# A mixer kernel's gated output projection, moved from a stage at the end into the scan loop

## What is computed

```
xz = x_seq @ W_in
x, z = (xz[..., :D_INNER], xz[..., D_INNER:])
x = _silu(_causal_conv(x, conv_w, conv_b))
proj = x @ W_xproj
dt = jax.nn.softplus(proj[..., :DT_RANK] @ W_dt + b_dt)
y = _selective_scan(x, dt, Bm, Cm, A, D)
return y * _silu(z) @ W_out
```

## Time and profile before

| | |
|---|---|
| median of 3 runs | 6110.16 us (6106.02 to 6110.85) |
| the profiled execution | 6104.23 us |
| its span | 6102.4 us |
| DVE busy | 5353.6 us, 88% of the span |
| POOL busy | 4946.7 us, 81% |
| PE busy | 4730.4 us, 78% |
| ACT busy | 3221.6 us, 53% |
| mean granted clock of PE | 0.734 |
| DVE busy tenths in 40 slices | 3224729999999999999999999999999999999953 |
| DMA, mean | 172 GB/s |

### The profile page before, as it was taken

One profiled execution on the slowest core, in us unless ns is written; L12 is line 12 of the kernel. 1 busy time (PEld: TensorE's weight loads), 2 busy tenths in 40 slices (PEclk: granted clock), 3 DMA queues, 4 the chain that ended last, 5 costly groups with the idle time before them and its releaser, 6 DMA issues. The chain is left out here.

```text
span 6102.4 us, 74088 instructions
## 1 busy us (share of the span) xinstructions
PE 4730.4 (78%) x17356; PEld 1206.1 (20%) x17356; DVE 5353.6 (88%) x3584; ACT 3221.6 (53%) x5155; POOL 4946.7 (81%) x2339
## 2 busy tenths in 40 slices
PE   7999737777777777777777777777777777777788
PEld 6776211111111111111111111111111111111122
DVE  3224729999999999999999999999999999999953
ACT  1226635555555555555555555555555555555533
POOL 0000429999999999999999999999999999999965
PEclk9999877666666666666666666666666676666689
DMA  1002745555555555555555555555555555555599
GB/s 34 27 27 82 224 122 182 183 183 183 183 181 182 181 180 179 184 179 182 180 182 180 181 181 182 181 181 181 182 183 183 183 183 183 183 183 183 183 263 273
DMA packets 351021, 1048.26 MB, mean 172 GB/s; under 512 B 66820, under 2 KB 101430, under 8 KB 300556
## 3 DMA queue, kind: packets, MB, share of 16 engines
q1 hardware_dynamic: 334976, 1022.36, 52.8%
q10 hardware_dynamic: 16012, 25.53, 1.3%
HBM read 836.01 MB, written 211.63 MB: 172 GB/s over the span
## 5 line engine op out<-in xcount | busy, mean ns | idle before, releaser
L1267 POOL TENSOR_TENSOR hc<-hring,c_rep 128x1024 f32<-128x1024 f32 x1539 | 3602.2, 2356 | 245.8 <-DVE hring L1230 235.2
L1230 DVE TENSOR_TENSOR_SCAN hring<-decay,carry,u_ps 128x1024 f32<-128x1024 f32 x1283 | 2971.8, 2333 | 0.0
L1035 PE MATMUL u_ps<-stack_b,w_spread 48*128 48x512 bf16 x2568 | 1117.4, 527 | 953.0 <-DVE hring L1230 951.8
L1125 ACT ACTIVATE decay<-dt_rep,w_a 128x1024 f32<-128x1024 f32 x1285 | 1469.8, 1146 | 571.0 <-DVE hring L1230 570.1
L1212 DVE TENSOR_TENSOR u_ps<-u_ps,u_rep 128x1024 f32<-128x1024 f32 x1284 | 1551.4, 1208 | 92.6 <-PE u_ps L1035 89.3
L1053 PE MATMUL y_ps<-hc,w_gather 128*32 128x512 f32 x6144 | 1170.8, 846 | 55.3 <-POOL hc L1267 55.3
L1125 ACT ACTIVATE u_ps<-dt_rep,w_a 128x1024 f32<-128x1024 f32 x257 | 287.4, 1118 | 979.4 <-DVE hring L1230 979.4
L1077 PE MATMUL prep_ps<-xn,w_conv 128*128 128x512 f32 x792 | 618.8, 875 | 73.0 <-DMA xn<-xn_scr 71.4
L1035 PEld LDWEIGHTS u_ps<-stack_b,w_spread 48*128 48x128 bf16 x2568 | 155.6, 102 | 2536.9 <-DVE hring L1230 1823.3
L582 POOL TENSOR_TENSOR xs<-xc_ln,rs 96x512 f32<-96x512 f32 x64 | 90.3, 1411 | 682.5 <-ACT rs L566 668.2
L1254 POOL TENSOR_TENSOR drive_p<-u_rep,b_rep 128x1024 f32<-128x1024 f32 x258 | 609.1, 2361 | 27.7 <-DMA u_rep<-u_scr 27.7
(11 more groups left out here) (108 smaller groups left out, 3926.8 us busy)
## 6 DMA issues: line engine op xcount, KB each, us to landing
dt_rep<-dt_scr SPq DMA_DIRECT2D x194, 1024.0 KB, 5.9
u_rep<-u_scr SPq DMA_DIRECT2D x194, 1024.0 KB, 7.9
c_rep<-bc_scr SPq DMA_DIRECT2D x260, 512.0 KB, 5.4
b_rep<-bc_scr SPq DMA_DIRECT2D x130, 512.0 KB, 4.4
xn<-xn_scr SPq DMA_DIRECT2D x132, 384.0 KB, 6.5
y_scr<-y_sb SPq DMA_DIRECT2D x768, 64.0 KB, 4.3
xn<-xn_scr SPq DMA_DIRECT2D x132, 256.0 KB, 6.7
dt_scr<-dt_sb SPq DMA_DIRECT2D x260, 128.0 KB, 2.1
```

The source lines that it names most:

```text
L1035: mm = nc.tensor.matmul(u_ps[nv % NSLOT][:, sl], w["spread"][:, q, :], upper(stack_b[drv][:, sl]), start=True, stop=True)
L1125: nc.scalar.activation(to[:, :], dt_rep[r][:, b, :], ACT.Exp, scale=w["a"][:, col:col + 1]).then_inc(decay_ready, 1)
L1230: nc.vector.tensor_tensor_scan(hring[nv % NHR][:, ::step], factor[:, ::step], term[:, ::step], carry[:, drv, nv:nv + 1], ALU.mult, ALU.add ...
L1267: nc.gpsimd.tensor_tensor(hc[nv % NHC][:, :], hring[nv % NHR][:, :], c_rep[q][:, :], ALU.mult).then_inc(c_applied, 1)
```

## The change

The scan loop gets two more tasks, `gate` and `slice`. In pass p (from p = 8, so from the second image on) they make one slice of the previous image's output: 56 slices in the passes 8 to 63. At step 14 of pass p-1 SP issues seven loads of slice p-8 (L1062 to L1066 of the new file; 983 KB). At steps 21 and 22 PE makes z into `prep_ps` and ACT copies it to `z_sb`. In pass p, at step 0 ACT takes the silu of z, at step 1 DVE adds the two y, at step 3 DVE multiplies, at step 7 PE projects (four float32 matmuls of 256 columns), at step 8 ACT copies the result and at step 10 SP stores it. The slice is laid out as 128 partitions by 768, as the scan's own channels are. `CONV_AT` moves by one step, so that the projection may use `prep_ps` at steps 7 and 8. The loop is split: three iterations without the new tasks, one unrolled iteration with the first z, 28 iterations with all of it. `output` keeps its form but runs over the last image's eight slices only (`over_last`). `weights` gains two matrices, with five more loads, a memset and three copies. The core of the diff:

```diff
-        CONV_AT = ((8, 9, 10), (12, 13, 14), (16, 17, 18))
+        CONV_AT = ((9, 10, 11), (13, 14, 15), (17, 18, 19))
...
+        SLICE_AT, Z_AT = 14, (21, 22)
+        SUM_Y_AT, GATE_AT, PROJECT_AT, RES_AT, OUT_STORE_AT = 1, 3, 7, 8, 10
+        SLICE_DMAS = 7
...
+        OUT_LAG = 2 * CHUNKS
+
+        def slice_of(it):
+
+            return it // CHUNKS - 1, (it + 1) % CHUNKS * T
...
+
+
+            with eng.Fori(0, CHUNKS - 1) as it:
+                iteration(it, (False, False), (False, False))
+            iteration(CHUNKS - 1, (False, True), (False, False))
+            with eng.Fori(CHUNKS, ITERS) as it:
+                iteration(it, (True, True), (True, True))
...
+                def gate(m, k, it, dr):
+                    if m == SLICE_AT:
+                        image, at = slice_of(it)
+                        at = at + dr * SL
+                        made, free, stored = ready(2 * k, k, 64 * NG * (k + OUT_LAG - 1))
+
+                        wait(sp, z_made, made, k)
+                        wait(sp, projected, free, k)
+                        sp.wait_ge(y_stored, stored)
+                        sp.dma_start(xz[:, :], d["xn_scr"][image, :, bass.ds(at + HALO, SL)]).then_inc(slice_in, 16)
+                        for to, scr in ((y_fwd, d["y_scr"][0]), (y_bwd, d["y_scr"][1])):
+                            sp.dma_start(to[:, 0:SL], scr[image, 0:P, bass.ds(at, SL)]).then_inc(slice_in, 16)
+                            for s in range(2):
+                                sp.dma_start(to[64 * s:64 * s + 64, SL:], scr[image, P:DI, bass.ds(at + s * (SL // 2), SL // 2)]).then_inc(slice_in, 16)
+
+                def slice_out(m, k, it, dr):
+                    if m == OUT_STORE_AT:
+                        image, at = slice_of(it)
+                        made, = ready(k + 1)
+                        sp.wait_ge(res_ready, made)
+                        sp.dma_start(d["out"][image, :, bass.ds(at + dr * SL, SL)], res[:, :]).then_inc(out_stored, 16)
+
+                run(sp, ("front", front), ("prep", prep), ("conv", conv), ("back", back), ("gate", gate), ("slice", slice_out))
...
                             wait(pe, prep_out, NPREP * pn + g, not isinstance(pn, int) or pn + g > 0)
+                            if g == 0 and slicing:
+                                pe.wait_ge(res_ready, pn - 1 - OUT_LAG)
...
+                def gate(m, k, it, dr):
+                    if m == Z_AT[0]:
+                        pe.wait_ge(slice_in, 16 * SLICE_DMAS * (k + 1))
+
+                        pe.wait_ge(prep_out, NPREP * (k + OUT_LAG + 1) + 3)
+                        nc.tensor.matmul(prep_ps[:, :], w["z"][:, 0:P], xz[:, :], start=True, stop=True).then_inc(z_made, 1)
+                    if m == Z_AT[1]:
+                        pe.wait_ge(z_out, 2 * k + 1)
+                        for s in range(2):
+                            mm = nc.tensor.matmul(prep_ps[64 * s:64 * s + 64, 0:SL // 2], w["z"][:, P:DI], xz[:, s * (SL // 2):(s + 1) * (SL // 2)],
+                                                  start=True, stop=True)
+                        mm.then_inc(z_made, 1)
+
+                def slice_out(m, k, it, dr):
+                    if m == PROJECT_AT:
+                        pe.wait_ge(gated, k + 1)
+
+                        pe.wait_ge(prep_out, NPREP * (k + OUT_LAG + 2))
+                        for s in range(2):
+                            cols = slice(s * (SL // 2), (s + 1) * (SL // 2))
+                            nc.tensor.matmul(prep_ps[0:C, cols], w["out"][:, 0, :], y_bwd[:, cols], start=True, stop=False)
+                            mm = nc.tensor.matmul(prep_ps[0:C, cols], w["out"][:, 1 + s, :], y_bwd[:, SL:], start=False, stop=True)
+                        mm.then_inc(projected, 1)
+
+                run(pe, ("front", front), ("back", back), ("prep", prep), ("slice", slice_out), ("conv", conv), ("gate", gate))
...
                         nc.scalar.activation(xa[dr][:, :], xc[:, :], ACT.Silu).then_inc(silu_done, 1)
+                        if slicing:
+                            act.wait_ge(z_out, 2 * (pn - OUT_LAG))
+                            nc.scalar.activation(z_sb[:, :], z_sb[:, :], ACT.Silu).then_inc(z_silu, 1)
                         load_exp_ln(nc)
...
+                def gate(m, k, it, dr):
+                    if m == Z_AT[0]:
+                        wait(act, gated, k, k)
+                        act.wait_ge(z_made, 2 * k + 1)
+                        nc.scalar.copy(z_sb[:, 0:SL], prep_ps[:, :]).then_inc(z_out, 1)
+                    if m == Z_AT[1]:
+                        act.wait_ge(z_made, 2 * k + 2)
+                        nc.scalar.copy(z_sb[:, SL:], prep_ps[:, 0:SL // 2]).then_inc(z_out, 1)
+
+                def slice_out(m, k, it, dr):
+                    if m == RES_AT:
+                        act.wait_ge(projected, k + 1)
+                        wait(act, out_stored, 16 * k, k)
+                        nc.scalar.copy(res[:, :], prep_ps[0:C, :]).then_inc(res_ready, 1)
...
-                run(dve, ("front", front))
+                def slice_out(m, k, it, dr):
+                    if m == SUM_Y_AT:
+                        dve.wait_ge(slice_in, 16 * SLICE_DMAS * (k + 1))
+                        nc.vector.tensor_tensor(y_fwd[:, :], y_fwd[:, :], y_bwd[:, :], ALU.add).then_inc(y_sum, 1)
+                    if m == GATE_AT:
+                        dve.wait_ge(y_sum, k + 1)
+                        dve.wait_ge(z_silu, k + 1)
+                        nc.vector.tensor_tensor(y_bwd[:, :], y_fwd[:, :], z_sb[:, :], ALU.mult).then_inc(gated, 1)
+
+                run(dve, ("front", front), ("slice", slice_out))
...
-                over_slices(sp, (0, load))
+                        sp.dma_start(t[:, r, :, :], src[B - 1, :, sl].rearrange("(h c) t -> c h t", h=2)).then_inc(o_loaded[r], 16)
+                    sp.dma_start(xz[:, r, :], d["xn_scr"][B - 1, :, HALO + s * SL:HALO + (s + 1) * SL]).then_inc(o_loaded[r], 16)
+
+                over_last(sp, (0, load))
```

More of the change, by code:

```diff
@@ L88, in over_slices, with over_last @@
     image(B - 1, last=True)
+def over_last(eng, *stages):
+    most = max(lead for lead, _ in stages)
+    for s in range(-most, NS):
+        for lead, what in stages:
+            if 0 <= s + lead < NS:
+                what(s + lead)
 def after(eng, sem, count):
@@ L634, in weights @@
             loads.append((wx[rows, col, :], d["w_x"][lo:hi, h, :]))
+            loads.append((out_w[rows, col, :], d["w_out"][lo:hi, h, :]))
             for k, name in enumerate(("conv_b", "dt_b", "skip")):
@@ L846, in run, with iteration @@
                         what(n, n, 0, 0)
-            with eng.Fori(0, ITERS) as it:
+            def iteration(it, gates, slices):
                 for dr in range(2):
@@ L858, in run @@
                             elif kind == "prep":
-                                what(m, p + 1, it + dr, 1 - dr)
-                            else:
-                                what(m, p + 2, it + 1, dr)
+                                what(m, p + 1, it + dr, 1 - dr, slices[dr])
+                            elif kind == "conv":
+                                what(m, p + 2, it + 1, dr, slices[dr])
+                            elif kind == "gate" and gates[dr]:
+                                what(m, p + 1 - OUT_LAG, it + dr, 1 - dr)
+                            elif kind == "slice" and slices[dr]:
+                                what(m, p - OUT_LAG, it, dr)
                     for kind, what in tasks:
@@ L1135, in front @@
                         if nv == 0:
-                            wait(act, carried, 2 * itv + drv, not isinstance(v, int))
+                            wait(act, carried, 2 * itv + drv, not isinstance(v, int) or v >= UNITS)
                         end = T - 1 if drv == 0 else 0
@@ L1219, in scan_unit @@
                     if nv == 0:
-                        wait(dve, carried, 2 * itv + drv, not isinstance(v, int))
+                        wait(dve, carried, 2 * itv + drv, not isinstance(v, int) or v >= UNITS)
                     step = 1 if drv == 0 else -1
@@ L1392, in _, with multiply @@
-                over_slices(act, (3, gate), (0, store))
+                    act.wait_ge(res_ready, s + 1)
+                    act.dma_start(d["out"][B - 1, :, s * SL:(s + 1) * SL], res[:, r, :]).then_inc(o_stored[r], 16)
+                over_last(act, (3, gate), (0, store))
             @block.vector
             def _(dve):
-                def multiply(b, s):
+                def multiply(s):
                     r = s % R
-                    dve.wait_ge(y_sum, NS * b + s + 1)
-                    dve.wait_ge(z_silu, NS * b + s + 1)
-                    after(dve, projected, NS * b + s - R + 1)
+                    dve.wait_ge(y_sum, s + 1)
+                    dve.wait_ge(z_silu, s + 1)
+                    after(dve, projected, s - R + 1)
```

99 lines of the change are left out of this document (58 added, 41 removed).

## The result

The changed kernel takes **6261.01 us** (median of 4 runs, 6259.72 to 6272.93), the kernel before 6108.77 beside it: a ratio of **1.0253**, interval 1.0241 to 1.0266. Slower, as forecast, by almost twice what was forecast: 152 us against 83. The profiled execution spans 6257.9 us, 155.5 more than before.

What follows compares the result with a forecast made beforehand. DVE was taken to set the scan's pace: 6104.2 - 222 saved + 3 once + 308 (5.5 us a pass times 56) = 6193 us. Its own range was 6131 to 6260; 8 in 10, 5990 to 6320.

Steps and rivals of the forecast that it cites:

- DVE's add and multiply: Steps 1 and 3 on DVE: each operation costs 1.0 us including waiting for POOL, 2.0 us a pass.
- rival 3: POOL keeps the port: the add waits for two more POOL instructions, 4.7 us more a pass, 6456 us; chance 0.07.
- The removed wait: DVE's wait for PE at 3076.23 goes because DVE comes there 1 us later: -0.1 us a pass.
- The projection: Step 7: four extra PE matmuls make drive 13 wait, 1.6 us a pass; bounds 0 and 2.4.
- First convolution group: One step later, its third piece shares step 11 with other PE work before drive 17: 0.3 us a pass.
- Third group: At step 19 a convolution piece comes before unit 1's spread, lengthening drive 1's wait: 1.1 us a pass; bounds 0 and 2.0.
- stack_b: Seven loads ahead of its load on SP make it late for PE's spread of unit 0: 0.6 us a pass.
- The output stage: Stage after the scan shrinks from 269.8 us to 48 us with eight slices left: 222 us saved; bounds 219 and 226.
- Once-only: Weights-stage loads, four DVE instructions there and two more loop entries: 3 us in all; bounds 0 and 10.
- half the passes: At step 19 about half the passes must have PE's clock at 1.00, with room for the convolution piece.
- the signs that the prediction named: Stage 48 us; DVE idle 3.7 us a pass at drives 13 and 1; unit 0's spread waits for stack_b; pass 82.3.
- Rival 1: PE keeps up with the extra matmuls; a pass costs only DVE's own 2.0 us, total 5997 us; chance 0.20.

Runs made afterwards that it cites:

- the last kernel: Against the kernel with all three alterations: the add on GpSimd at step 0 and VectorE's multiply at step 4 instead of 3; 5981.66 us, ratio 0.9791.
- the kernel with all three alterations: Changed kernel with loads issued at step 16, third convolution group back at steps 16 to 18, projection split over steps 7 and 8; 5981.58 us, ratio 0.9791.

## Why the prediction was right on the side and short on the size

- **DVE's add and multiply, 2.0 a pass**: 1.95. The turn that POOL keeps (rival 3, 6456) did not come in the changed kernel, where POOL's instruction ended 0.17 to 0.29 us after the operation's start. That it exists is shown by the add on GpSimd, one turn long, and by the eight passes of the last kernel, where that end came a little later, 0.42 to 0.49 us after the start. So it stayed away by luck of the phase, and not for the reason that the prediction gives ("DVE takes the port at once").
- **The removed wait, -0.1**: the wait at 3076.23 is that of drive 8, 0.10 of the 0.17 a pass, and it is gone in the passes with a slice; right, and too small to matter.
- **The projection, 1.6**: 1.32 at drive 13, and 83 us when it was taken away alone, 1.48 a pass. Right.
- **First convolution group, 0.3**: 0.14 at drive 17. Right.
- **Third group, 1.1, and stack_b, 0.6**: this is the step that failed. I added the two as terms of their own, 1.7, and they are one: drives 0 and 1 wait 3.11 a pass, and the loads alone, moved, gave back 3.68 (drive 13's wait also fell by 0.3), while the group alone on the kernel before costs 0.4. Two sizes were wrong in it. I took SP's issues at 3.2 us, by four stores' 1.81; the seven took 4.5 to the next issue (median; 4.68 in the pass shown). And I put "half the passes" at the full clock at step 19. In the kernel before it was 36 of 55 (chain 2.54 us against 4.69); in the changed kernel it was none.
- **The output stage, 222**: 224.8, the stage 45 us and not 48. Right.
- **Once-only, 3**: 15, of which 6.2 before the first drive (2.0 to 7.8 in the other kernels with the same weights stage, so in part scatter) and 6.8 in the first eight passes, which make no slice and which I had counted as unchanged. The convolution is late there too; on the kernel before that alone made them 2.5 longer. The rest is not accounted for.

In all 5.5 us a pass was forecast and 6.5 came, 57 us of the 68 between 6193 and 6261; the once-only part has 12, and the output stage gave 3 back. The pass lies inside the forecast's own 4.4 to 6.7, the time 1 us beyond its 6131 to 6260, and well inside the range for 8 in 10. Of the signs that the prediction named, the place of PE's waits (drives 13 and 1), the wait for stack_b's load and the stage of 48 us came true; the wait at drive 0 was not among them. Rival 1 (5997, "PE keeps up") described no state of this kernel but a neighbour of it: with the waits gone the kernel with all three alterations has 1.70 a pass where the rival had 2.0, and 5982 us.

By the Trainium skill (TensorE: Matmul & The Clock Gate, "HAM oscillation — how this bites in real kernels") gaps in PE's work bring the low clock. At step 19 the traces agree only in part. In the kernel before, all 19 steady passes with a pause of 3.25 or 3.26 us had a gather of 1.93 us behind it; with the loads moved, 17 passes with the same pause had one of 1.07. I had let the rule speak only for a rival, and it would have warned of what a late load can cost; but by the length of the pause alone nothing here could have been forecast.

## What to carry to other kernels

Before loads are put on a queue, read from the trace what that engine issues next and how soon it is needed: each issue took 0.33 to 0.60 us, and seven in front of a critical load cost 212 us (133 where the third group had been moved back), though the load took no longer to land. Behind it, or in the queue of an engine with slack, they were free. Terms that end in the same wait are to be worked out as one chain, at either level of the clock, and not added.

## What the runs showed of the hardware

The same chain on TensorE (spread, gather, skip term, one convolution piece) took 3.55 us at the full clock and up to 6.59 at the low one. A pause of 3.25 us ahead of it was followed by the low clock in one kernel and by the full one in another. Nor did work without a pause bring the full clock soon. Busy time by window, the kernel before, columns as in the earlier trace rows:

```profile
5082.00:5100.00 18.00, 18.00 (x44) 3.19 (x48) 17.99 (x12) 13.13 (x21) 17.92 (x11) 0.50 0.49 142
```

PE was busy in all of the 18 us, at a granted clock of 0.50. What sets the level is open.

VectorE's operation on two SBUF operands and GpSimd's instructions shut each other out, and who comes next isn't the one who has waited longest. An end of a GpSimd instruction up to 0.3 us after the VectorE operation's start let the full add and multiply in (0.93 to 1.11 us, the next GpSimd instruction 0.7 longer), in every pass. Ends that came 0.42 to 0.49 and 1.08 to 1.55 us after it passed it over, and the next end let it in (3.5 to 3.6 and 4.2 to 4.7 us), in 62 of 64 cases. The multiply cut to 8 columns was passed over once in 56 at 0.30 (2.63 us). So the phase goes with the outcome but doesn't decide it alone. What does is open: no run varies the phase by itself, or separates it from whether GpSimd's next instruction had yet to wait for a scan. VectorE's scans were not touched by it (2.33 us beside GpSimd's in every kernel).
